# Halved norms for the first group, and scores 4 to 7 in another order and other banks

## The reference

```
scores = einsum('btd,bsd->bts', K, K) * tril           # K is the context, per batch of 64
x = x + tanh(g_xattn) * (Q + scores @ Q)               # Q = layernorm(x), no softmax
n = layernorm(x)
shared = silu(n @ shared_w1.T) @ shared_w2.T           # hidden 512
top 2 of 8 experts by n @ gate_w.T, softmax of the two logits as gates
selected = sum over the two experts of gate * (silu(n @ w1[e].T) @ w2[e].T)
x = x + tanh(g_ffn) * (shared + selected)
```

## Time and profile before

| | us |
|---|---|
| median of 3 runs (228.19 to 228.93) | 228.3 |
| the profiled execution, its own time | 228.44 |
| its span in the profile | 226.6 |
| PE busy | 220.6 (97%) |
| PEld busy | 191.6 (85%) |
| POOL busy | 147.6 (65%) |
| ACT busy | 133.0 (59%) |
| DVE busy | 118.0 (52%) |

### The profile page before, as it was taken

The page is one execution under the profiler, slowest core; times in us unless marked ns, Lnnn a source line. Parts: engine busy times, 40 slices in busy tenths (PEclk is TensorE's granted clock), DMA queues, the critical chain, the costliest instruction groups (busy, mean ns, idle before and its releaser), DMA issues.

```text
span 226.6 us, 5999 instructions
## 1 busy us (share of the span) xinstructions
PE 220.6 (97%) x1728; PEld 191.6 (85%) x1731; DVE 118.0 (52%) x546; ACT 133.0 (59%) x304; POOL 147.6 (65%) x178
## 2 busy tenths in 40 slices
PE   7989999999999999999999999999999999999993
PEld 2754867786777789999999999999999999999793
DVE  6899998856864589995203210221122102466214
ACT  2649896597475555655565556545654565466510
POOL 4772875767777777777777777777744544465600
PEclk9999999999999999999999999999999999999998
DMA  6899210211245995867774266777777776999633
GB/s 233 263 392 392 66 54 33 64 52 52 68 98 156 260 285 161 228 185 183 197 202 151 72 196 202 215 238 223 219 244 220 200 228 187 271 355 370 238 95 127
DMA packets 30478, 43.47 MB, mean 192 GB/s; under 512 B 4992, under 2 KB 16512, under 8 KB 30192
## 3 DMA queue, kind: packets, MB, share of 16 engines
q1 hardware_dynamic: 25264, 32.87, 49.0%
q0 software_dynamic: 4320, 9.41, 11.4%
q10 hardware_dynamic: 864, 0.80, 1.0%
HBM read 30.45 MB, written 12.62 MB: 190 GB/s over the span
## 4 chain that ended last, share of the span: by engine, by line
PE 90%; DMA 3%; DVE 2%; ACT 1%; POOL 1%; issue 1%; POOLq 0%; SPq 0%; DVEq 0%; ACTq 0%
PE bank L1343 28%; PE bank L1364 28%; PE bank L1191 11%; PE bank L1204 10%; PE bank L1317 3%; PE bank L1138 3%; PE bank L1145 2%; DMA y_rows<-y,dest 2%; PE bank L1122 2%; PE bank L1211 2%; PE bank L1155 1%; DMA q<-y_rows 1%; PE bank L1115 1%; POOL rstd L492 0%; POOL y_rows L557 0%
## 5 line engine op out<-in xcount | busy, mean ns | idle before, releaser
L557 POOL DMA_INDIRECT y_rows<-y,dest x71 | 69.7, 982 | 36.6 <-ACT y L733 25.1
L531 POOL DMA_INDIRECT expert_rows<-n,slot x64 | 62.8, 981 | 24.3 <-issue 18.3
L1364 PE MATMUL bank<-w,hT 128*128 x568 | 74.5, 275 | 0.0
L1343 PE MATMUL bank<-xT,w_ring 128*128 128x128 f32 (+1 forms) x432 | 74.1, 309 | 0.0
L1364 PEld LDWEIGHTS bank<-w,hT 128*128 128x128 f32 x568 | 71.3, 192 | 1.6
L727 ACT ACTIVATE hT<-bank 128x512 f32<-128x512 f32 x71 | 42.4, 597 | 34.3 <-PE bank L1343 34.2
L1343 PEld LDWEIGHTS bank<-xT,w_ring 128*128 128x128 f32 x432 | 59.3, 192 | 2.0 <-issue 0.2
L1024 DVE COPY xT<-bank 128x512 f32<-128x512 f32 (+2 forms) x19 | 12.4, 653 | 72.3 <-PE bank L1317 72.3
L733 ACT ACTIVATE y<-bank,gate 128x128 f32<-128x128 f32 x71 | 26.1, 368 | 21.3 <-PE bank L1364 20.9
L1204 PEld LDWEIGHTS bank<-sw,sT 128*128 128x128 f32 x224 | 27.4, 192 | 5.3 <-issue 5.0
L1191 PE MATMUL bank<-nT,sw 128*128 128x512 f32 x56 | 28.7, 609 | 0.0
(11 more groups left out here) (154 smaller groups left out, 198.1 us busy)
## 6 DMA issues: line engine op xcount, KB each, us to landing
w_ring<-in_w1T SPq DMA_DIRECT2D x54, 256.0 KB, 3.6
x_ring<-expert_rows SPq DMA_DIRECT2D x37, 72.5 KB, 2.8
x_ring<-expert_rows SPq DMA_DIRECT2D x17, 145.0 KB, 3.7
w<-in_w2T SPq DMA_DIRECT2D x2, 1024.0 KB, 11.8
kT<-y_rows SPq DMA_DIRECT2D x8, 256.0 KB, 6.5
nT<-y_rows SPq DMA_DIRECT2D x7, 256.0 KB, 4.5
out<-xres SPq DMA_DIRECT2D x7, 256.0 KB
xres<-in_xP SPq DMA_DIRECT2D x3, 512.0 KB, 7.1
```

Source lines behind the costliest of these rows:

```text
L531: pool.indirect_dma_start(out=x_dram[:, :], out_offset=bass.IndirectOffsetOnAxis(ap=slot[:, i, k:k + 1], axis=0), in_=n[:, i, :], in_offse ...
L557: pool.indirect_dma_start(out=y_dram[:, :], out_offset=bass.IndirectOffsetOnAxis(ap=dest[:, b:b + 1], axis=0), in_=y[:, j], in_offset=None ...
L1343: last = pe.matmul(ps_up(b)[:, j * width:(j + 1) * width], w1_ring[:, w % W_RING, c * P:(c + 1) * P], xT[:, s % X_SETS, i * P:i * P + widt ...
L1364: last = pe.matmul(ps_y(b), hidden(b, c), w2[:, ds(at + c * D, D)], start=(c == 0), stop=(c == HC - 1))
```

## The change

`first_norm` makes the norms of group 0, of both stages, in two halves of two tiles each, with a pow on [128, 2] and a signal for each half; ACT's two halves of q and n wait for one half each (`steps_to`). The routing constants are made in two parts, `position_constants` ahead of the second stage's norm of group 0 and the rest behind norm1 of group 2. Scores 5, 6 and 7 change banks, and those copied by ACT are 4 and 7 instead of 4, 5 and 6. On PE score 4 goes ahead of apply 1, score 5 is the one interleaved with the transpositions, score 6 takes the place of the warm matmul, and score 7 goes from behind shared_up 3 to ahead of apply 2. SP issues the context of group 7 two places earlier.

```diff
--- before.py
+++ after.py
@@ -212,8 +212,8 @@
 
         bank = [stack.enter_context(nc.psum_tensor(f"bank{i}", [P, 512], f32)) for i in range(8)]
         ps_q, ps_n = bank[1], bank[2]
-        ps_s = [bank[0], bank[4], bank[7], bank[5], bank[0], bank[7], bank[4], bank[7]]
-        COPIED = (4, 5, 6)
+        ps_s = [bank[0], bank[4], bank[7], bank[5], bank[0], bank[7], bank[0], bank[4]]
+        COPIED = (4, 7)
         ps_warm = bank[3]
         ps_logit, ps_pos = bank[3][:, 3 * P:3 * P + G * STRIP], bank[3][:, G * E:(1 + PARTS) * G * E]
         ps_strips = bank[2][:, 0:P]
@@ -322,8 +322,8 @@
         def last_cols(half):
             return slice(LAST * GW + half * GW // 2, LAST * GW + (half + 1) * GW // 2)
 
-        def in_range(g):
-            return 0 <= g < GROUPS
+        def steps_to(g, half):
+            return g + 2 if g else half + 1
 
         def masked(g):
             return scores[:, g] if g < 2 else hT[:, g - 2]
@@ -361,9 +361,9 @@
             load_context(4)
             sp.dma_start(sw1[:, :], sw1T).then_inc(sw_in, 16)
             load_context(5)
+            load_context(6)
             load_tokens(3)
             sp.dma_start(sw2[:, :], sw2T).then_inc(sw2_in, 16)
-            load_context(6)
             load_tokens(4)
             for half in range(2):
                 cols = slice(half * E * H // 2, (half + 1) * E * H // 2)
@@ -487,10 +487,16 @@
                                        base=-S, pattern=[[0, P - S]], channel_multiplier=1))
             pool.memset(unused[:, 0:1], 0.0).then_inc(consts_ready, 1)
 
-            def norm(slot_kind, done):
+            def norm(slot_kind, done, some=slice(0, G)):
                 slot, kind = slot_kind
-                chained(pool.tensor_tensor(rstd[:, slot, kind], var_eps[:, slot, kind], minus_half[:, :], ALU.pow))
-                pool.tensor_tensor(shift[:, slot, kind], neg_mean[:, slot, kind], rstd[:, slot, kind], ALU.mult).then_inc(done, 1)
+                chained(pool.tensor_tensor(rstd[:, slot, kind, some], var_eps[:, slot, kind, some], minus_half[:, some], ALU.pow))
+                pool.tensor_tensor(shift[:, slot, kind, some], neg_mean[:, slot, kind, some], rstd[:, slot, kind, some],
+                                   ALU.mult).then_inc(done, 1)
+
+            def first_norm(slot_kind, stats_done, done):
+                pool.wait_ge(stats_done, 1)
+                for half in range(2):
+                    norm(slot_kind, done, slice(half * G // 2, (half + 1) * G // 2))
 
             def norm1(g):
                 pool.wait_ge(stats1_done, g + 1)
@@ -500,13 +506,15 @@
                 pool.wait_ge(stats2_done, g + 1)
                 norm(second(g), shift2_done)
 
-            def routing_constants():
+            def position_constants():
                 chained(pool.memset(before[:, :], 1.0))
                 chained(pool.affine_select(out=before[:, :], in_=before[:, :], compare_op=ALU.is_gt, fill=0.0,
                                            base=0, pattern=[[1, P]], channel_multiplier=-1))
                 chained(pool.memset(ones[:, :], 1.0))
                 chained(pool.affine_select(out=not_before[:, :], in_=ones[:, :], compare_op=ALU.is_ge, fill=0.0,
                                            base=0, pattern=[[-1, P]], channel_multiplier=1))
+
+            def routing_constants():
                 chained(pool.iota(n[:, :, ID], pattern=[[1, TILES]], base=0, channel_multiplier=TILES,
                                   allow_small_or_imprecise_dtypes=True))
                 chained(pool.iota(expert_row[:, :], pattern=[[1, E]], base=0, channel_multiplier=0,
@@ -533,11 +541,12 @@
                                         in_=n[:, i, :], in_offset=None).then_inc(x_scattered[stage_of(g, k)], 16)
 
 
-            norm1(0)
+            first_norm(first(0), stats1_done, shift1_done)
             norm1(1)
+            position_constants()
+            first_norm(second(0), stats2_done, shift2_done)
+            norm1(2)
             routing_constants()
-            norm2(0)
-            norm1(2)
             norm1(3)
             block_constants()
             norm2(1)
@@ -578,7 +587,7 @@
             def centre_and_scale(g, half):
                 slot, kind = first(g)
                 if g < GROUPS // 2:
-                    act.wait_ge(shift1_done, g + 1)
+                    act.wait_ge(shift1_done, steps_to(g, half))
                 else:
                     act.wait_ge(pairs_done, g // 2 - 1)
                 at_least(act, attn_psum, g - 1)
@@ -589,7 +598,7 @@
             def normalise(g, half):
                 slot, kind = second(g)
                 if g < POWERS2:
-                    act.wait_ge(shift2_done, g + 1)
+                    act.wait_ge(shift2_done, steps_to(g, half))
                 else:
                     act.wait_ge(pairs_done, g // 2)
                 for t in range(half * G // 2, (half + 1) * G // 2):
@@ -631,6 +640,7 @@
             tanh_gates()
             centre_and_scale(1, 0)
             centre_and_scale(1, 1)
+            copy_scores(4)
             normalise(0, 0)
             normalise(0, 1)
             evacuate_nT(0)
@@ -638,12 +648,10 @@
             evacuate_strips(0)
             centre_and_scale(2, 1)
             shared_silu(0)
-            copy_scores(4)
             centre_and_scale(3, 0)
-            copy_scores(5)
             shared_silu(1)
+            copy_scores(7)
             shared_silu(2)
-            copy_scores(6)
             shared_silu(3)
             normalise(1, 0)
             normalise(1, 1)
@@ -1144,7 +1152,7 @@
                     pe.wait_ge(n_done, G * g + t + 1)
                     last = pe.transpose(ps_n[:, t * P:(t + 1) * P], n[:, g * G + t, 0:D], ident[:, :])
                     if g == 0:
-                        score_tile(6, t)
+                        score_tile(5, t)
                 last.then_inc(nT_psum, 1)
 
             def logit_strips(g):
@@ -1217,21 +1225,20 @@
             score(2)
             apply_scores(0)
             score(3)
+            score(4)
             apply_scores(1)
-            score(4)
-            score(5)
-            start_score(6)
+            start_score(5)
             transpose_n(0)
-            keep_warm(1)
+            score(6)
             logit_strips(0)
             shared_up(0)
             logits(0)
             shared_up(1)
+            score(7)
             apply_scores(2)
             shared_up(2)
             positions(0)
             shared_up(3)
-            score(7)
             shared_down(0, 0)
             shared_down(0, 1)
             transpose_n(1)
```

## The result

The changed kernel took 229.72 us (median of 11, 229.06 to 231.25), the kernel before 228.49 in runs taken beside it (median of 11, 228.12 to 229.16): 1.006 times as long, with a 95% interval of 1.0034 to 1.0086. It is slower by about 1.2 us, and the interval excludes no change. The executions of the changed kernel fall into two groups, parted by TensorE's mean granted clock. Seven have 0.998 or more and a median of 229.33; four have 0.990 to 0.993 and a median of 230.95.

A forecast was written before the change was run, and what follows sets the result against it. It took TensorE, busy 220.6 of 226.6 us, as the bound; −0.13 (strips), −0.36 (positions, up-projection 3) and +0.95 (uncovered silu) made +0.46, taken as +0.4: 228.3 + 0.4 = 228.7 us, own range 228.4 to 229.0, overall 227.9 to 229.4.

The forecast's parts named there:

- Part 3: TensorE around the first transpositions: idles about 1.0 until 13.49, score 6 replaces the warm matmul, strips at 16.56, 0.13 gained.
- the sum: Total at the first down-projection: −0.13 strips, −0.36 positions and up-projection 3, +0.95 uncovered silu, making +0.46, taken as +0.4.
- Part 1: First q in halves on GpSimd and ACT: q done at 8.7 instead of 9.05, application of scores 0 0.10 shorter.
- Part 4: Score 7 ahead of apply 2: 0.36 back at positions 0 and up-projection 3, but 0.95 idle before the down-projection.
- Part 1, pow: GpSimd's pow for the first norm's halves: 0.60 on 128x2, between bounds of 0.20 and 1.01.
- Rival A: GpSimd's pow doesn't get shorter on 128x2: strips 0.75 later than forecast, 229.4 us; chance 0.15.
- Part 1, q: ACT's first q finished at 8.7 instead of about 9.05; application of scores 0 loses 0.10 of pacing by q.
- Rival D: TensorE's clock falls in the longer idle of 1.0 before the transpositions, losing 1 to 2 us: 230; chance 0.03.
- B: GpSimd's pow at its lower bound of 0.20: n 0.4 earlier, 228.3 us, no change; chance 0.07.
- C: The first down-projection isn't held because the fourth silu is released during up-projection 3: 227.8 us, faster; chance 0.08.
- E: DVE's half microsecond of delay is exposed at positions 1 or n of group 2: 229.2 us; chance 0.05.

The follow-up runs named there:

- e1: The changed kernel again, no edit, for a second profile; 1.0051 times the kernel before, 4 of 12 executions at a low clock.
- e3: The changed kernel with score 7 back behind up-projection 3, banks of scores 5 and 7 exchanged, ACT copying 4 and 5; 1.0027 times the kernel before.
- e11: The kernel before with the halves and score 7 ahead of apply 2, old order of scores 4 to 6 and warm matmul kept; 1.0017 times the kernel before.
- e10: The kernel before with only the new order of scores 3 to 6, its banks and copies, without halves, score 7 in its old place; 1.0016 times the kernel before.
- e2: The changed kernel with two warm matmuls put into the wait ahead of the first transposition; 1.0072 times the kernel before.
- e6: The changed kernel with the removed warm matmul back, between the transpositions and score 6; 1.0053 times the kernel before.
- e4: The kernel before with only the halves of the first norms; 1.0001 times the kernel before.
- e7: The kernel before with the halves, DVE's statistics of group 4 behind placing group 0, ACT's copy of scores 5 behind the second silu; 1.0022 times the kernel before.
- e9: The changed kernel with four warm matmuls ahead of the transpositions and one behind them; 1.0032 times the kernel before, median 229.64 us.
- e12: The changed kernel with four warm matmuls ahead of the transpositions, one behind, and score 7 back behind up-projection 3; 1.001 times the kernel before, 228.95 us.
- e5: The kernel before without its one warm matmul between the transpositions and the logit strips; 0.9991 times the kernel before.

## Why the prediction was wrong

It forecast 228.7, +0.4 and so no change, and put 0.03 on the fall of the clock. Measured beside the kernel before are +1.23. Of this 0.84 is paid at full clock (229.33 − 228.49), about twice the forecast, and 0.39 (229.72 − 229.33) is what the executions with a fallen clock add to the median. Two steps failed. Part 3 took the "idles about 1.0 until 13.49" as free, with the clock's fall at 0.03; and the sum has the strips at −0.13, where e1 has them at +0.19 (16.88 − 16.69), because of two errors in Part 1. Point by point:

- **Part 4, the uncovered silu: right.** Between strips and down-projection e1 has 23.81 − 16.88 = 6.93, and the prediction 23.49 − 16.56 = 6.93. That the two agree to 0.01 is luck: up-projection 3 starts 0.07 later behind the strips than forecast (5.14 for 5.07), and PE resumes 0.05 after the silu, not 0.13. Positions 0 don't wait, and the row that it asked for is there, 0.69 for sT. Taking it back is worth 0.64 (e3), and done alone with the halves it costs 0.4 (e11).
- **Part 1, pow: the size was off.** It was 0.70 on 128x2, not 0.60; of the 0.81 by which the pow exceeds the multiply, 0.31 go with half of the columns. Rival A (1.01) is out, and by the rows the cost is neither fixed nor proportional. The Trainium skill, GPSIMD Engine Reference, Performance versus the Vector engine, gives about 2.6 cycles per element for a tensor_tensor, from an add, and no figure for pow. By it, as an estimate, two columns fewer save some 5 cycles, next to nothing; the multiply agrees (0.20 and 0.19), the pow, with its 0.31, doesn't.
- **Part 1, q: a bound was missed.** With q earlier, the application of scores 0 is entered when score 2 is done, and score 2 waits for the context of groups 2 and 3. In e1 it starts at 7.59 and the application at 8.53, where it was 8.34; the first transposition is at 13.84, not 13.49: 0.10 by pow, 0.25 by this. I read what q released and not what PE's queue held in front of it. The size changes from one execution to the next: in the profile of the first section score 2 starts at 7.32 and the transposition is at 13.59, so there the 0.10 of pow is all. In all ten profiles with the halves the first transposition follows the start of score 2 by 6.19 to 6.31; in the kernel before (7.41 and 7.12) and e10 (7.18) it is at 14.00 to 14.01 whatever score 2 does.
- **Part 3: score 6 behind the transpositions, right in length** (13.84 to 16.88 is 3.04, forecast 3.07), with the two errors above carried on: strips at 16.88 instead of 16.56. In e1's profile that makes 0.46 + 0.32 = 0.78 at the down-projection, and the executions at full clock took 0.84 (229.33 − 228.49) and 0.91 (e1) more than the kernel before. So nothing later absorbs it, as forecast.
- **Rival D: the step of Part 3 that failed.** I took "idles about 1.0 until 13.49" as free, because it is over before anything waits for PE, and called the work after it the same. In the changed kernel and e1 the clock fell in 8 of 23 executions, in e2, e3 and e6 in 10 of 27. The new order of scores 3 to 6 does it by itself (e10, 5 of 12); halves and score 7 don't (e4, e7, e11: 0 of 36); with the wait filled it doesn't happen (e9, e12: 0 of 21). What doesn't fit is the one low execution in 12 of e5, in the old order without its warm matmul.
- **D's price of 1 to 2 us was right for most such executions**: 230.95 − 229.33 = 1.6 here, 1.0 to 1.8 in e1, e2, e6 and e10 where the mean clock is 0.990 to 0.993, but only 0.6 to 0.9 in three of e3, 2.2 in e5's, and 2.2 to 3.7 where it is 0.985. In the traces 25.02 − 13.59 = 11.43 from first transposition to down-projection stands against 23.81 − 13.84 = 9.97 in e1. Its 230 was too low (they took 230.69 to 231.25), since the 0.84 comes on top, and its chance, 0.03, was far off.
- The Trainium skill, TensorE: Matmul & The Clock Gate, HAM oscillation, gives the rule by which D was named, that gaps between matmuls can bring the half-rate clock back. The traces agree: the fall follows the 1.09 of idle. By the profiles the idle time before the transpositions goes with it: it is 1.08 to 1.34 in the changed kernel, e1, e3, e6 and e10 and 0.52 in e2, all of which fall in some executions, and at most 0.22 in the kernel before, e4, e7, e9, e11 and e12, none of which does in 173. e9 (0 of 9), the changed kernel but for the five warm matmuls, shows that filling the hole ends the fall, and e10 that the order, with its banks and copies, brings it. How much filling it takes, and why one execution falls and the next doesn't, stays open.
- **Rivals B, C and E** didn't come: pow is far above 0.20, the silu starts only when the up-projection ends, and positions 1 follow at 36.59 in e1, 0.79 later than in the earlier trace rows, without a wait. DVE's fullness did matter, in e4 and e7, but not for this change.

## What to carry to other kernels

Where the engine that sets the end idles before a step, its idle time need not be free even when nothing is late: look at the granted clock behind it in several executions, and fill the hole or keep the work there. Before a filler between two steps is moved, ask what it hides at its old place; here a score of 0.95 hid a silu, and moving it uncovered 0.7. Look at all executions with their granted clock, not at a median alone: a cost that hits one in three is told apart only so. And before an idle time is taken from a profile, count the instructions that the code issues there: a missing record reads as a wait.

## What the runs showed of the hardware

- TensorE's granted clock fell from 2.4 to 1.2 GHz in about a third of the executions of one program. In the three profiles that show it, it fell between 15 and 17 us and stayed low for about 3.4 us twice (mean clock of the execution 0.993 and 0.991) and for 6.8 us once (0.985).
- A GpSimd pow takes 1.01 us on 128x4 and 0.70 on 128x2, a multiply 0.20 and 0.19.
- The load of the context of groups 2 and 3, issued at 1.7 in every profile, landed 5.2 to 5.9 us after its issue in the ten profiles with the halves and 5.3 to 5.5 in the four without them. These ranges overlap, so no link with the halves is shown; the spread of 0.7 reaches the first transposition where the halves are in.
